# The tokenizer of a vision tower: patches that the host lays out transposed, against patches that the kernel normalises and transposes itself

## The chip, the cores and the metric

The kernel runs on one core of a Trainium2 chip. The metric is the device time of one execution in microseconds. The core's engines are named as the profile names them: PE is TensorE's matmul, PEld its weight load, DVE is VectorE, ACT is ScalarE, POOL is GpSimd, SP is the engine that issues the transfers (DMA). PSUM is the memory of eight banks that PE writes.

## The reference

Sixty-four images of 96 x 96 x 3 are cut into 36 patches of 16 x 16 each, so 2304 tokens; then come three attention layers and a sparse feed-forward layer, which are not touched here. The part at issue is the tokenizer:

```
x5 = concat([x] + shifts(x))            # the image and four copies shifted by one pixel
tokens = patchify(x5, 16)               # 16*16*3*5 = 3840 features a token
mu, var = mean(tokens), mean((tokens - mu)**2)
h = ((tokens - mu) * rsqrt(var + 1e-3) * gamma + beta) @ W + b     # W: 3840 x 192
```

A token and its shifts read one window of 18 x 18 pixels, 972 numbers, each of which occurs in 1, 3, 4 or 5 of the five copies (its count). So the projection over 3840 features can be done over 972 window numbers with a weight that is the sum of five shifted, gamma-scaled weights, and mean and variance are sums over the window weighted by the count.

## The kernel before

The program is one launch in five phases, A to E; `phase_end` makes every engine wait for the other four at the end of each. Phase A is the tokenizer, `phase_tokenizer`. Each engine has a function of its own there (`load` for SP, `vector`, `scalar`, `gpsimd`, `tensor`), works in the order in which it is written, and waits on semaphores.

Before, the tokens of three images (108) are one group, there are 24 groups laid out (22 are real), and six groups are a chunk. The host lays out whole rows of 18 pixels per row of patches (`A_xraw`, 108 partitions, one token row a partition; four transfers, two buffers). For each chunk and each of the six window positions w:

- DVE (`means`, L304) multiplies the window with the counts and sums it; after six of them one small instruction (L310) makes the means.
- ACT (`statistics`, L368) squares the centred window; DVE (`variances`, L320) sums the squares with the counts. There are two buffers of squares, so these two take turns. Ln and Exp (L374, L378) make the reciprocal deviation.
- POOL (L403) normalises the window into `A_xn`, PE transposes it in nine pieces (L427), ACT copies three pieces at a time into `A_xT` (`copies`, L386), and PE projects a group of 108 tokens in nine products (L438). DVE adds the bias (`evacuate`, L329) and writes `h`, which stays on the chip.

Ahead of that, DVE folds the five shifted weights into one (L339, L342: 9 + 36 instructions) while PE multiplies beta with them for the bias (L413, 45 products). In DVE's order this stands behind chunk 0's statistics and ahead of chunk 1's; in PE's order ahead of all transposes. Each fp32 product is two PE records and two PEld records in the trace.

Of the kernel before, what the change touches and what calls it, by code (L numbers as in the profile page):

```python
# [236 lines left out]
def phase_tokenizer(nc, ctx, sem, plan, bank, h, ident, ones, loaded, weights_at):  # L237
# [4 lines left out]
    xraw = [plan(f"A_xraw{s}", [GT, WIN * ROW]) for s in range(2)]  # L242
    xn = [plan(f"A_xn{s}", [GT, WSIZE]) for s in range(3)]
    xT = [plan(f"A_xT{s}", [GT, KT, GT, PER_SIDE]) for s in range(2)]
    count = plan("A_count", [GT, WSIZE])

    sums = [plan(f"A_sums{s}", [GT, 5, PER_SIDE]) for s in range(2)]
    gb = plan("A_gb", [GT, 2, SHIFTS * KT])
    wtok = plan("A_wtok", [GT, KT, DIM])
    bias_bc = plan("A_bias_bc", [GT, DIM])  # L250
    tok_b = plan("A_tok_b", [1, DIM])
    bias_row = plan("A_bias_row", [1, DIM])
    squares = [plan(f"A_squares{s}", [GT, WSIZE]) for s in range(2)]
    scratch = plan("A_scratch", [GT, WSIZE], BF16)
    w5 = plan("A_w5", [GT, SHIFTS, KT, DIM])

    p.ones_set = sem("A_ones_set")
    s_sum, s_mean, s_sq, s_var, s_log, s_rstd = (sem("A_" + n) for n in ("sum", "mean", "sq", "var", "log", "rstd"))
    s_xn, s_T, s_Tev, s_out, s_h = (sem("A_" + n) for n in ("xn", "T", "Tev", "out", "h"))
    s_w, s_bias, s_bias_sb = sem("A_w"), sem("A_bias"), sem("A_bias_sb")  # L260
    slot_load = [loaded["tokx0"], loaded["tokx1"]]
    tbank = bank[0:4]
    obank = bank[4:6]
    bbank = bank[6]

    def window(x, w):

        return x[:, :].rearrange("p (r c) -> p r c", c=ROW)[:, :, PATCH * CHANNELS * w:PATCH * CHANNELS * w + WROW]

    def as_window(t):  # L270
        return t[:, :].rearrange("p (r c) -> p r c", c=WROW)

    def load(sp, ins):
        sp.dma_start(xraw[0][:, :], ins["x"][0]).then_inc(slot_load[0], 16)
        sp.dma_start(count[:, :], ins["count"]).then_inc(loaded["tokc"], 16)
        sp.dma_start(gb[:, :, :], ins["tok_gb"]).then_inc(loaded["tokw"], 16)
        sp.dma_start(tok_b[:, :], ins["tok_b"]).then_inc(loaded["tokw"], 16)
        for k in range(SHIFTS):
            sp.dma_start(w5[:, k], ins["tok_w"][:, k]).then_inc(loaded["tokw"], 16)
            if k == 1:  # L280
                sp.dma_start(xraw[1][:, :], ins["x"][1]).then_inc(slot_load[1], 16)
        for c in range(2, CHUNKS):
            sp.wait_ge(s_xn, PER_SIDE * (c - 1))
            sp.wait_ge(s_sq, PER_SIDE * (c - 1))
            sp.dma_start(xraw[c % 2][:, :], ins["x"][c]).then_inc(slot_load[c % 2], 16)

    def vector(dve):
        dve.wait_ge(loaded["tokc"], 16)  # L290

        def means(c):
            t = sums[c % 2]
            dve.wait_ge(slot_load[c % 2], 16 * (c // 2 + 1))
            for w in range(PER_SIDE):
                if c >= 2:
                    dve.wait_ge(s_rstd, c - 1)

                n = c * PER_SIDE + w
                if n:  # L300
                    dve.wait_ge(s_sum, n)
                    if c:
                        dve.wait_ge(s_var, c * PER_SIDE)
                dve.scalar_tensor_tensor(out=as_window(scratch), in0=window(xraw[c % 2], w), scalar=1.0,  # L304
                                         in1=as_window(count), op0=ALU.mult, op1=ALU.mult,
                                         accum_out=t[:, 0, w:w + 1]).then_inc(s_sum, 1)
            dve.wait_ge(s_sum, PER_SIDE * (c + 1))
            if c >= 2:
                dve.wait_ge(s_xn, PER_SIDE * (c - 1))
            dve.tensor_scalar(t[:, 1, :], t[:, 0, :], -1.0 / FEATS, None, ALU.mult).then_inc(s_mean, 1)  # L310

        def variances(c):
            for w in range(PER_SIDE):
                n = c * PER_SIDE + w
                if w:
                    evacuate(c - 2, w - 1)
                dve.wait_ge(s_sq, n + 1)
                if n:
                    dve.wait_ge(s_var, n)
                dve.scalar_tensor_tensor(out=as_window(scratch), in0=as_window(squares[n % 2]), scalar=1.0,  # L320
                                         in1=as_window(count), op0=ALU.mult, op1=ALU.mult,
                                         accum_out=sums[c % 2][:, 2, w:w + 1]).then_inc(s_var, 1)

        def evacuate(c, j):
            if c < 0:
                return
            n = c * CHUNK_GROUPS + j
# [1 line left out]
            dve.tensor_tensor(h[:, n, :], obank[n % 2][0:GT, 0:DIM], bias_bc[:, :], ALU.add).then_inc(s_h, 1)  # L329

        means(0)
        variances(0)

        dve.wait_ge(loaded["tokw"], 16 * (2 + SHIFTS))
        for k in range(SHIFTS):
            for t in range(KT):
                scale = gb[:, 0, k * KT + t:k * KT + t + 1]
                if k == 0:
                    dve.tensor_scalar(wtok[:, t, :], w5[:, 0, t, :], scale, None, ALU.mult).then_inc(s_w, 1)  # L339
                else:  # L340
                    dve.wait_ge(s_w, (k - 1) * KT + t + 1)
                    dve.scalar_tensor_tensor(out=wtok[:, t, :], in0=w5[:, k, t, :], scalar=scale,  # L342
                                             in1=wtok[:, t, :], op0=ALU.mult, op1=ALU.add).then_inc(s_w, 1)
        dve.wait_ge(s_bias, 1)
        dve.tensor_copy(bias_row[:, :], bbank[0:1, 0:DIM]).then_inc(s_bias_sb, 1)
        dve.wait_ge(s_bias, 2)
        dve.tensor_copy(bias_bc[:, :], bbank[0:GT, 256:256 + DIM]).then_inc(s_bias_sb, 1)
        dve.wait_ge(s_bias_sb, 2)
        means(1)
        variances(1)  # L350
        for c in range(CHUNKS):
            if c + 2 < CHUNKS:
                means(c + 2)
                variances(c + 2)
                evacuate(c, CHUNK_GROUPS - 1)
            else:
                for j in range(CHUNK_GROUPS):
                    evacuate(c, j)

    def scalar(act):  # L360
        def statistics(c):
            t = sums[c % 2]
            act.wait_ge(s_mean, c + 1)
            for w in range(PER_SIDE):
                n = c * PER_SIDE + w
                if n >= 2:
                    act.wait_ge(s_var, n - 1)
                act.activation(as_window(squares[n % 2]), window(xraw[c % 2], w), ACT.Square,  # L368
                               bias=t[:, 1, w:w + 1]).then_inc(s_sq, 1)
                if c:  # L370
                    copies(c - 1, w)
# [1554 lines left out]
```

## Time and profile before

| | |
|---|---|
| median of 3 runs | 1573.12 us (1569.11 to 1573.88) |
| the profiled execution: its time, its span | 1564.85 us, 1562.7 us |
| phase A in it | 0 to 185.65 us |
| busy over the span: PE, DVE, ACT, POOL | 82%, 64%, 60%, 29% |
| granted TensorE clock, mean | 0.92 of full speed |

The span is first to last instruction of the profiled execution; the time of that execution holds a little more. Rows of the trace give a start in us from the span's beginning, a duration, the engine, the kernel's line, and what was written from what. "idle before" is how long the engine stood still ahead of an instruction, and what released it.

### The profile page before, as it was taken

What the parts mean: (1) busy time and instruction counts of PE and PEld (TensorE: products, weight loads), DVE (VectorE), ACT (ScalarE), POOL (GpSimd) and SP (SyncE); (2) the same over time, 40 slices, a digit from 0 to 9 for tenths busy, and PEclk for the clock granted to TensorE, in tenths of its full rate; (3) what the DMA queues carried; (4) which work ended last, traced back from release to release, by engine and by line L of the source; (5) the groups of instructions that cost most, each with busy time, mean ns of one, the idle gap of its engine ahead of it and who ended that gap; (6) DMA issues with size and microseconds to landing.
All of it is one profiled execution on the core that took longest, in us unless ns stands there. A gap on an engine that the chain in (4) does not pass through costs nothing.

```text
span 1562.7 us, 27926 instructions
## 1 busy us (share of the span) xinstructions
PE 1282.7 (82%) x9582; PEld 1164.6 (75%) x9582; DVE 999.2 (64%) x2455; ACT 943.8 (60%) x3298; POOL 458.7 (29%) x447
## 2 busy tenths in 40 slices
PE   1688777778768999999977999999984128999999
PEld 0387776667757888898966888888872117999998
DVE  5663255544546999999866788888875773333333
ACT  2445177777855889889875888888873102222233
POOL 0132100210203233233203334343413304555555
PEclk9688899899977999999998999999996558999999
DMA  5130100020000000000000000000002100000000
GB/s 233 59 117 1 51 12 1 1 62 1 1 1 1 2 1 1 2 1 2 2 10 1 2 1 2 2 1 1 2 2 81 61 0 1 10 1 10 10 10 12
DMA packets 7040, 30.09 MB, mean 19 GB/s; under 512 B 1603, under 2 KB 4400, under 8 KB 5560
## 3 DMA queue, kind: packets, MB, share of 16 engines
q1 hardware_dynamic: 6902, 28.31, 5.6%
q8 instruction: 79, 1.29, 0.3%
q14 instruction: 59, 0.48, 0.1%
HBM read 26.54 MB, written 1.77 MB: 18 GB/s over the span
## 4 chain that ended last, share of the span: by engine, by line
PE 39%; DVE 24%; ACT 4%; issue 3%; POOL 1%; POOLq 0%; ACTq 0%; DVEq 0%
PE bank L1344 4%; DVE t_ss L734 4%; DVE f_eq L1625 4%; DVE t_p L772 3%; PE bank L1370 3%; PE bank L1332 2%; DVE t_raw L750 2%; DVE t_ss L731 2%; PE bank L1312 2%; PE bank L1689 2%; PE bank L1691 2%; PE bank L1704 2%; PE bank L1692 2%; PE bank L1690 2%; PE bank L1693 2%
## 5 line engine op out<-in xcount | busy, mean ns | idle before, releaser
L1164 ACT ACTIVATE t_p<-bank,t_nmax 108x108 f32<-108x108 f32 x792 | 267.4, 355 | 47.6 <-DVE t_nmax L754 46.0
L754 DVE TENSOR_REDUCE t_nmax<-bank 108x4 f32<-108x432 f32 x198 | 119.5, 604 | 141.8 <-PE bank L1344 141.5
L1810 POOL TENSOR_TENSOR f_hid_lo<-f_hid,f_hid_hi 128x432 fp32r<-128x432 f32 (+2 forms) x144 | 145.9, 1014 | 173.5 <-ACT f_hid_hi L1796 173.5
L1013 POOL TENSOR_TENSOR t_sq<-t_raw 108x768 f32<-108x768 f32 x88 | 139.9, 1591 | 181.1 <-ACT t_raw L1104 180.7
L1344 PEld LDWEIGHTS bank<-t_kT,t_qT 128*108 128x108 f32 x1584 | 187.2, 179 | 2.7
L1344 PE MATMUL bank<-t_kT,t_qT 128*108 128x108 f32 x1584 | 187.1, 262 | 0.0
L1766 DVE SCALAR_TENSOR_TENSOR f_hid<-bank,f_maskT 128x432 f32<-128x432 f32 (+2 forms) x144 | 80.2, 557 | 166.9 <-PE bank L1693 165.7
L1796 ACT CAST f_hid_hi<-f_hid 128x432 fp32r<-128x432 f32 (+2 forms) x144 | 73.9, 513 | 182.4 <-DVE f_hid L1766 182.3
L1164 ACT ACTIVATION_READ_ACCUMULATOR t_p<-bank,t_nmax 108x1 f32 x792 | 167.0, 211 | 0.0
L772 DVE TENSOR_TENSOR t_p<-t_p,t_rinv 108x432 f32<-108x432 f32 x198 | 148.9, 752 | 6.8
L1353 PE MATMUL bank<-ident,t_p 108*108 108x108 f32 x792 | 109.6, 261 | 32.6 <-ACT t_xt L1085 28.2
L1021 POOL TENSOR_TENSOR t_xl<-t_xt,t_xh 128x108 fp32r<-128x108 f32 x44 | 18.7, 425 | 330.2 <-DVE t_xh L721 272.4
L1353 PEld LDWEIGHTS bank<-ident,t_p 108*108 108x108 f32 x792 | 82.0, 134 | 44.8 <-ACT t_xt L1085 31.8
L1172 ACT COPY t_pT<-bank 108x432 f32<-108x432 f32 x198 | 99.4, 522 | 16.3 <-PE bank L1353 14.6
L750 DVE TENSOR_TENSOR t_raw<-t_raw,t_rn 108x768 f32<-108x768 f32 x88 | 85.1, 966 | 31.3 <-ACT t_rn L1131 29.1
L1332 PE MATMUL bank<-ident,t_raw 108*128 108x108 f32 x528 | 80.0, 261 | 23.9 <-DVE t_raw L750 11.1
L1104 ACT COPY t_raw<-bank 108x384 f32<-108x384 f32 x176 | 86.3, 493 | 16.0 <-PE bank L1316 15.9
L1332 PEld LDWEIGHTS bank<-ident,t_raw 108*128 108x128 f32 x528 | 62.6, 142 | 42.3 <-ACT t_pT L1172 30.1
L1370 PE MATMUL bank<-t_pT,t_v 108*64 108x108 f32 (+1 forms) x1584 | 86.0, 267 | 1.8 <-issue 1.8
L438 PE MATMUL bank<-A_wtok,A_xT 108*108 108x192 f32 x432 | 81.2, 349 | 6.7 <-ACT A_xT L386 6.7
L1534 PE MATMUL bank<-f_small,f_halves 128*128 128x1 f32 x68 | 19.8, 362 | 78.0 <-DVE f_eq L1625 70.2
L438 PEld LDWEIGHTS bank<-A_wtok,A_xT 108*108 108x108 f32 x432 | 76.0, 188 | 8.5 <-ACT A_xT L386 4.8
(224 smaller groups left out, 3487.6 us busy)
## 6 DMA issues: line engine op xcount, KB each, us to landing
A_xraw<-in_x SPq DMA_DIRECT2D x4, 2232.6 KB
A_w<-in_tok_w SPq DMA_DIRECT2D x5, 729.0 KB
f_raw_down<-in_w_proj SPq DMA_DIRECT2D x1, 2304.0 KB, 8.7
out_tokens<-h SPq DMA_DIRECT2D x21, 81.0 KB
f_raw<-in_w_mfc SPq DMA_DIRECT2D x1, 1536.0 KB, 6.9
f_raw<-in_w_mfc SPq DMA_DIRECT2D x2, 768.0 KB, 11.9
W_raw<-in_wC SPq DMA_DIRECT2D x1, 1159.0 KB
W_raw<-in_wC SPq DMA_DIRECT2D x2, 579.5 KB
```

Source lines behind the costliest of these rows:

```text
L438: mm = pe.matmul(obank[n % 2][0:GT, 0:DIM], xT[c % 2][:, t, rows * j:rows * (j + 1), :].rearrange("p a b -> p (a b)"), wtok[:, t, :], star ...
L750: dve.tensor_tensor(v, v, r, ALU.mult).then_inc(s["qn"], 1)
L754: dve.tensor_reduce(b.nmax[:, 4 * c:4 * c + 4], self.sbank[(3 * g + c) % 2][0:GT, 0:4 * GT].rearrange("p (a n) -> p a n", n=GT), AX.X, ALU ...
L772: dve.tensor_tensor(p, p, b.rinv[:, sl].unsqueeze(2).to_broadcast([GT, 4, GT]), ALU.mult).then_inc(s["pn"], 1)
L1013: pool.tensor_tensor(b.sq[:, 768 * m:768 * m + 768], v, v, ALU.mult).then_inc(s["sq"], 1)
L1164: act.activation(b.p[g % 2][:, m, :], self.sbank[(3 * g + c) % 2][0:GT, n * GT:(n + 1) * GT], ACT.Exp, bias=b.nmax[:, m:m + 1], accum_out= ...
L1172: act.copy(b.pT[:, 4 * c:4 * c + 4, :], src.rearrange("p (a n) -> p a n", a=4)).then_inc(s["Tev"], 1)
L1332: mm = pe.transpose(o, b.raw[k][:, 128 * (3 * u + n):128 * (3 * u + n + 1)], I[0:GT, 0:GT])
L1344: mm = pe.matmul(o[0:GT, n * GT:(n + 1) * GT], b.qT[g % 2][:, hd, :], b.kT[g % 2][:, hd // self.per_tile, :], start=False, stop=True, skip ...
L1353: mm = pe.transpose(t[0:GT, n * GT:(n + 1) * GT], b.p[g % 2][:, 4 * c + n, :], I[0:GT, 0:GT])
L1370: mm = pe.matmul(self.pv[n][lo:hi, t * GT:(t + 1) * GT], b.v[g % 4][:, self.vd * hd:self.vd * (hd + 1)], b.pT[:, hd, :], start=True, stop= ...
L1810: pool.tensor_tensor(self.hid_lo[m % 4][:, c], self.hid[m % 4][:, c], self.hid_hi[m % 4][:, c].bitcast(F32), ALU.subtract).then_inc(s["lo" ...
```

## The change

The host now lays the windows out transposed: window numbers on 121 partitions, eight to a partition (960 of the 972 occur at all, since the window's corners never do; padded to 968 so that all eight numbers of a partition have the same count), tokens along the free dimension, and only the 22 real groups. `A_x` has a buffer for each of six batches (4, 4, 4, 4, 3 and 3 groups), so no load waits for a buffer. Nothing is normalised ahead of the projection:

- `load`: small constants, five weight loads, six batches; the constants `ident`, `owner`, `other` come behind them. The two casts of `owner` and `other` move behind phase A.
- `tensor`: 40 products for the bias and the column sums of the weights (L357), one more (L358), two that spread the results over partitions (L360, L361); then for each group eight products of the raw patches with the weights, 193 columns wide (L370; the last column gives the mean), and one product of one column that sums the squares (L374).
- `vector`: 40 instructions fold the weights (L285, L288), one fills the mean's column (L290), one copies the two rows (L292), one subtracts the weights' column mean, so that the mean of the patch drops out (L295), one copies the bias (L297). For each batch one reduction adds the eight squares of a partition (L304). For each group: copy of mean and mean square (L309), variance (L311), and out of PSUM: times reciprocal deviation plus bias (L316).
- `scalar`: one Square for each batch, which writes in the order of tokens, so with a step of 32 bytes (L335); Ln and Exp for each group (L341, L343).
- `gpsimd`, the transposes, their copies and `A_xraw`, `A_xn`, `A_xT`, `A_count` are gone. `h` shrinks by two groups.

```diff
+BATCHES = [4, 4, 4, 4, 3, 3]
+WT = 8
+WROWS = 121
...
+        pA.load(sp, ins)
         for dst, name in ((ident, "ident"), (owner_f, "owner"), (other_f, "other")):
             sp.dma_start(dst[:, :], ins[name]).then_inc(loaded["const"], 16)
-        pA.load(sp, ins)
...
+        pA.vector(dve)
+        phase_end(dve, "A")
         dve.wait_ge(loaded["const"], 48)
         dve.tensor_copy(owner[:, :], owner_f[:, :]).then_inc(cast_done, 1)
         dve.tensor_copy(other[:, :], other_f[:, :]).then_inc(cast_done, 1)
-        pA.vector(dve)
-        phase_end(dve, "A")
...
+    ld_x = [loaded["tokx0"], loaded["tokx1"], loaded["tokx2"], loaded["tokx2"], loaded["tokx3"], loaded["tokx3"]]
+    of_x = [16, 16, 32, 32, 32, 32]
...
+        dve.scalar_tensor_tensor(out=w[:, :, 0:DIM], in0=wbank[0:WROWS, 0:DIM].unsqueeze(1).to_broadcast([WROWS, WT, DIM]),
+                                 scalar=seen[:, 1:2], in1=w[:, :, 0:DIM], op0=ALU.mult, op1=ALU.add).then_inc(s_w, 1)
...
+        def sum_squares(u):
+            n = BATCHES[u] * GT
+            dve.wait_ge(s_sq, u + 1)
+            if u >= 2:
+                dve.wait_ge(s_out, sum(BATCHES[:u - 1]))
+            dve.tensor_reduce(sums[u % 2][:, 0:n], squares[u % 2][:, 0:n, :], AX.X, ALU.add).then_inc(s_sum, 1)
...
+        dve.wait_ge(s_bias, 1)
+        sum_squares(0)
+        for n, (u, j) in enumerate(groups):
+            if j == 1 and u + 1 < len(BATCHES):
+                sum_squares(u + 1)
+            statistics(n)
+            if n:
+                finish(n - 1)
+        finish(GROUPS - 1)
...
+            act.wait_ge(ld_x[u], of_x[u])
+            if u >= 2:
+                act.wait_ge(s_sum, u - 1)
+            act.activation(squares[u % 2][:, 0:n, :].rearrange("p n t -> p t n"), x[u][:, :, :], ACT.Square)\
+               .then_inc(s_sq, 1)
...
+        square(0)
+        square(1)
+        for n, (u, j) in enumerate(groups):
+            root(n)
+            if j == 1 and u + 2 < len(BATCHES):
+                square(u + 2)
...
+        pe.wait_ge(s_w, CENTRED)
+        for n, (u, j) in enumerate(groups):
+            o, cols = obank[n % 4], slice(j * GT, (j + 1) * GT)
             if j == 0:
+                pe.wait_ge(ld_x[u], of_x[u])
+            if n >= 4:
+                pe.wait_ge(s_h, n - 3)
+            for t in range(WT):
+                pe.matmul(o[0:GT, 0:DIM + 1], x[u][:, t, cols], w[:, t, :], start=(t == 0), stop=(t == WT - 1),
+                          skip_group_check=True)
+            if j == 0:
+                pe.wait_ge(s_sum, u + 1)
+            pe.matmul(o[0:GT, DIM + 1:DIM + 2], sums[u % 2][:, cols], seen[:, 0:1], start=True, stop=True,
+                      skip_group_check=True).then_inc(s_out, 1)
```

PE's order at the start of the program before: the bias products, then all of chunk 0's transposes, then projections and the next chunk's transposes by turns (an x behind a row counts equal neighbours; the figures are rows by columns of the output).

```order
L413 MATMUL bank<-A_w_89,A_gb 1x192 x45
L414 MATMUL bank<-A_tok_b,ones 1x192
L416 MATMUL bank<-A_bias_row,ones 108x192
L427 MATMUL bank<-ident,A_xn_73 108x108 x9
L427 MATMUL bank<-ident,A_xn_74 108x108 x9
L427 MATMUL bank<-ident,A_xn_75 108x108 x9
L438 MATMUL bank<-A_wtok,A_xT_76 108x192 x9
```

The same place after; `A_x_72` and `A_x_73` are the first two batches, `A_sums` the squares summed by partition.

```order
L357 MATMUL bank<-A_w_71,A_gb 2x192 x40
L358 MATMUL bank<-A_tok_b,A_pick 2x192
L360 MATMUL bank<-A_rows,A_pick 128x192
L361 MATMUL bank<-A_rows,A_pick 108x192
L370 MATMUL bank<-A_w,A_x_72 108x193 x8
L374 MATMUL bank<-A_seen,A_sums_80 108x1
L370 MATMUL bank<-A_w,A_x_73 108x193 x8
L374 MATMUL bank<-A_seen,A_sums_81 108x1
```

No transpose is left between the projections, and each group ends in a product that needs DVE's sums. The last pair of rows is the second batch's first group; three more pairs of the first batch stand ahead of it.

ACT's order after, from its first square on: the third batch's square stands ahead of the Ln and Exp of groups 2 and 3.

```order
L335 ACTIVATE A_squares_78<-A_x_72 121x8x432
L335 ACTIVATE A_squares_79<-A_x_73 121x8x432
L341 ACTIVATE A_st_89<-A_st_89 108x1
L343 ACTIVATE A_st_89<-A_st_89 108x1
L341 ACTIVATE A_st_90<-A_st_90 108x1
L343 ACTIVATE A_st_90<-A_st_90 108x1
L335 ACTIVATE A_squares_78<-A_x_74 121x8x432
L341 ACTIVATE A_st_91<-A_st_91 108x1
```

DVE's order after, from the end of the weights to the second group: the sum of the first batch's squares stands behind the centring and the bias, the second batch's ahead of group 1's statistics.

```order
L288 SCALAR_TENSOR_TENSOR A_w<-A_w_71,A_gb,A_w 121x192 x32
L290 COPY A_w<-A_seen 121x8
L292 COPY A_rows<-bank 2x192
L295 SCALAR_TENSOR_TENSOR A_w<-bank,A_seen,A_w 121x8x192
L297 COPY A_bias<-bank 108x192
L304 TENSOR_REDUCE A_sums_80<-A_squares_78 121x432
L309 COPY A_st_89<-bank 108x2
L311 SCALAR_TENSOR_TENSOR A_st_89<-A_st_89 108x1
L304 TENSOR_REDUCE A_sums_81<-A_squares_79 121x432
```

So the weights, which before stood between two chunks' statistics, now come first on DVE, and nothing of the patches is touched ahead of them but ACT's squares.

## Rows read from the trace of the kernel before

**Rows 1.** The page: busy time, share of the span and instructions by engine.

```profile
PE 1282.7 (82%) x9582; PEld 1164.6 (75%) x9582; DVE 999.2 (64%) x2455; ACT 943.8 (60%) x3298; POOL 458.7 (29%) x447
```

**Rows 2.** Timeline where phase A ends: start, duration, engine, line.

```profile
170.67 0.36 DVE L329 TENSOR_TENSOR h<-bank,A_bias_bc 108x192 f32<-108x192 f32 x1 [5.04 <-PE bank L438]
...
185.29 0.36 DVE L329 TENSOR_TENSOR h<-bank,A_bias_bc 108x192 f32<-108x192 f32 x1 [2.57 <-PE bank L438]
185.76 2.02 POOL L527 MEMSET W_rawb<- 33x2318 f32 x1 [29.72 <-DVEq L130]
```

**Rows 3.** Phase A in three stretches: busy time, clock, DMA share, GB/s.

```profile
0.00:52.00 52.00, 18.86 (x105) 9.44 (x106) 31.09 (x76) 8.27 (x9) 3.75 (x7) 1.00 0.44 176
52.00:87.00 35.00, 19.54 (x94) 15.49 (x92) 25.64 (x36) 16.59 (x26) 11.84 (x7) 0.61 0.17 65
87.00:186.00 99.00, 85.58 (x546) 83.02 (x546) 32.24 (x64) 45.41 (x70) 18.14 (x15) 0.91 0.16 47
```

**Rows 4.** Longest waits in phase A: total, times, longest.

```profile
ACT A_squares L368 <- DVE A_sums L310: 71.0, 4, 29.5
DVE h L329 <- PE bank L438: 41.3, 14, 5.0
```

**Rows 5.** DMA share and rate in two stretches (engine columns as in rows 3).

```profile
20.00:30.00 10.00, 0.00 (x0) 0.00 (x0) 8.12 (x15) 6.68 (x7) 0.00 (x0) 1.00 0.74 310
190.00:192.00 2.00, 0.11 (x1) 0.14 (x2) 1.81 (x7) 0.41 (x2) 0.00 (x0) 0.50 1.01 427
```

**Rows 6.** DMA issues at the start, and one transfer's size and landing.

```profile
0.74 0.42 SPq L150 DMA_DIRECT2D ident<-in_ident  x1
3.74 0.97 SPq L279 DMA_DIRECT2D A_w<-in_tok_w  x2
...
ident<-in_ident SPq DMA_DIRECT2D x1, 64.0 KB, 1.7
```

**Rows 7.** The bias products (L413) on PE: first two windows, and all of them.

```profile
34.00:36.00 2.00, 2.00 (x8) 0.84 (x7) 1.00 0.02 4
40.00:42.00 2.00, 2.00 (x14) 1.01 (x12) 1.00 0.00 0
32.70 16.96 PE L413 MATMUL bank<-A_w,A_gb 108*1 108x192 f32 x90 [32.70 <-DMA A_w<-in_tok_w]
```

**Rows 8.** Two projections of nine products each, and the clock around the first.

```profile
86.00:90.00 4.00, 0.96 (x6) 0.72 (x6) 2.72 (x6) 2.66 (x4) 0.00 (x0) 0.79 0.00 0
90.30 5.50 PE L438 MATMUL bank<-A_wtok,A_xT 108*108 108x192 f32 x18
130.41 3.09 PE L438 MATMUL bank<-A_wtok,A_xT 108*108 108x192 f32 x18
```

**Rows 9.** Groups of instructions nearest in kind to the new ones, DVE.

```profile
L342 DVE SCALAR_TENSOR_TENSOR A_wtok<-A_w,A_gb,A_wtok 108x192 f32<-108x192 f32 x36 | 11.9, 404 | 0.0
L503 DVE SCALAR_TENSOR_TENSOR W_raw<-W_mean,W_raw 128x1536 f32<-128x1536 f32 x2 | 3.4, 1724 | 0.0
L499 DVE TENSOR_REDUCE W_mean<-W_raw 128x24 f32<-128x1536 f32 x2 | 3.4, 1719 | 0.0
L731 DVE TENSOR_REDUCE t_ss<-t_sq 108x12 f32<-108x768 f32 x44 | 41.4, 941 | 6.5 <-POOL t_sq L1013 6.5
L734 DVE TENSOR_REDUCE t_ss<-t_sq 108x64 f32<-108x768 f32 x44 | 65.4, 1486 | 6.5 <-POOL t_sq L1013 6.5
```

**Rows 10.** The same on ACT, and one row of PE.

```profile
L1570 ACT CAST f_wd<-f_raw_down 128x4608 fp32r<-128x4608 f32 x1 | 4.0, 4032 | 19.8 <-DMA f_raw_down<-in_w_proj 19.8
63.55 1.91 ACT L386 COPY A_xT<-bank 108x324 f32<-108x324 f32 x3
198.69 1.71 ACT L1149 COPY t_qT<-bank 32x324 f32<-32x324 f32 x4 [0.29 <-PE bank L1330]
L1069 ACT ACTIVATE t_rstd<-t_logv 108x1 f32<-108x1 f32 x66 | 13.4, 203 | 2.1
516.41 0.92 PE L1344 MATMUL bank<-t_kT,t_qT 128*108 128x108 f32 x8
```

More of the change, by code:

```diff
@@ L85, in build_in @@
     fixed = Plan(base)
-    h = fixed("h", [GT, GROUPS_LAID, DIM])
+    h = fixed("h", [GT, GROUPS, DIM])
     ident = fixed("ident", [128, 128])
@@ L131, in phase_end @@
         eng.wait_ge(done, block_engines * (phases.index(name) + 1))
-    pA = phase_tokenizer(nc, ctx, sem, Plan(region), bank, h, ident, ones, loaded, weights_at)
+    pA = phase_tokenizer(nc, ctx, sem, Plan(region), bank, h, ones, loaded)
     prep = weight_prep(nc, sem, Plan(staging_at), loaded, splitC, splitD)
@@ L168, in _ @@
     def _(pe):
-        pe.wait_ge(loaded["const"], 48)
         pA.tensor(pe)
         phase_end(pe, "A")
+        pe.wait_ge(loaded["const"], 48)
         pe.wait_ge(loaded["wB"], 16)
@@ L232, in _, with phase_tokenizer @@
         F.gpsimd_mlp(pool)
-def phase_tokenizer(nc, ctx, sem, plan, bank, h, ident, ones, loaded, weights_at):
+def phase_tokenizer(nc, ctx, sem, plan, bank, h, ones, loaded):
     class A:
@@ L241, in phase_tokenizer @@
     p = A()
[L242 to L271, printed above, removed]
+    w5 = plan("A_w5", [WROWS, SHIFTS, WT, DIM])
+    x = [plan(f"A_x{u}", [WROWS, WT, n * GT]) for u, n in enumerate(BATCHES)]
+    squares = [plan(f"A_squares{s}", [WROWS, BATCHES[0] * GT, WT]) for s in range(2)]
@@ new lines, in phase_tokenizer @@
+    sums = [plan(f"A_sums{s}", [WROWS, BATCHES[0] * GT]) for s in range(2)]
+    w = plan("A_w", [WROWS, WT, DIM + 1])
+    gb = plan("A_gb", [WROWS, SHIFTS * WT, 2])
+    seen = plan("A_seen", [WROWS, 2])
+    tok_b = plan("A_tok_b", [2, DIM])
+    pick = plan("A_pick", [2, 3, 128])
+    rows = plan("A_rows", [2, DIM])
+    bias = plan("A_bias", [GT, DIM])
+    st = [plan(f"A_st{s}", [GT, 5]) for s in range(4)]
+    s_w, s_rows, s_rows_sb, s_wide, s_bias, s_sq, s_sum = (sem("A_" + n) for n in (
+        "w", "rows", "rows_sb", "wide", "bias", "sq", "sum"))
@@ new lines, in phase_tokenizer, with weights_here @@
+    s_out, s_mu, s_var, s_log, s_rstd, s_h = (sem("A_" + n) for n in ("out", "mu", "var", "log", "rstd", "h"))
+    ld_w = [loaded["tokw0"], loaded["tokw1"], loaded["tokw2"]]
+    ld_x = [loaded["tokx0"], loaded["tokx1"], loaded["tokx2"], loaded["tokx2"], loaded["tokx3"], loaded["tokx3"]]
+    of_x = [16, 16, 32, 32, 32, 32]
+    obank = bank[0:4]
+    rbank, wbank = bank[4], bank[5]
+    groups = [(u, j) for u, n in enumerate(BATCHES) for j in range(n)]
+    CENTRED = SHIFTS * WT + 2
+    def weights_here(eng, k):
+        eng.wait_ge(ld_w[k // 2], 32 if k < 4 else 16)
@@ L273, in load @@
     def load(sp, ins):
[L274 to L277, printed above, removed]
+        for dst, name in ((gb[:, :, :], "tok_gb"), (seen[:, :], "tok_seen"), (tok_b[:, :], "tok_b"),
+                          (pick[:, :, :], "tok_pick")):
+            sp.dma_start(dst, ins[name]).then_inc(loaded["tokc"], 16)
@@ L278, in load @@
         for k in range(SHIFTS):
[L279 to L285, printed above, removed]
-    def vector(dve):
[L290 to L327, printed above, removed]
-            dve.wait_ge(s_out, n + 1)
[L329 to L334, printed above, removed]
-        for k in range(SHIFTS):
[L336 to L371, printed above, removed]
-            act.wait_ge(s_var, PER_SIDE * (c + 1))
-            act.activation(t[:, 3, :], t[:, 2, :], ACT.Ln, bias=1e-3, scale=1.0 / FEATS).then_inc(s_log, 1)
-            act.wait_ge(s_log, c + 1)
-            if c >= 2:
-                act.wait_ge(s_xn, PER_SIDE * (c - 1))
-            act.activation(t[:, 4, :], t[:, 3, :], ACT.Exp, scale=-0.5).then_inc(s_rstd, 1)
-        def copies(c, w):
-            for q in range(3):
-                n = (c * PER_SIDE + w) * 3 + q
-                act.wait_ge(s_T, n + 1)
-                if c >= 2:
-                    act.wait_ge(s_out, CHUNK_GROUPS * (c - 1))
-                act.copy(xT[c % 2][:, 3 * q:3 * q + 3, :, w],
-                         tbank[n % 4][0:GT, 0:3 * GT].rearrange("p (t n) -> p t n", t=3)).then_inc(s_Tev, 1)
-        statistics(0)
-        for c in range(1, CHUNKS):
-            statistics(c)
-        for w in range(PER_SIDE):
-            copies(CHUNKS - 1, w)
@@ new lines, in scalar, with square, root @@
+    def scalar(act):
+        def square(u):
+            n = BATCHES[u] * GT
+            act.wait_ge(ld_x[u], of_x[u])
[3 more added lines that the diff above has]
+               .then_inc(s_sq, 1)
+        def root(n):
+            t = st[n % 4]
+            act.wait_ge(s_var, n + 1)
+            act.activation(t[:, 3:4], t[:, 2:3], ACT.Ln, bias=1e-3, scale=-1.0).then_inc(s_log, 1)
+            act.wait_ge(s_log, n + 1)
+            act.activation(t[:, 4:5], t[:, 3:4], ACT.Exp, scale=-0.5).then_inc(s_rstd, 1)
+        square(0)
[4 more added lines that the diff above has]
+                square(u + 2)
@@ new lines, in tensor @@
+    def tensor(pe):
+        pe.wait_ge(loaded["tokc"], 64)
+        for k in range(SHIFTS):
+            weights_here(pe, k)
+            for t in range(WT):
+                pe.matmul(rbank[0:2, 0:DIM], gb[:, k * WT + t, :], w5[:, k, t, :], start=(k + t == 0), stop=False)
+        pe.matmul(rbank[0:2, 0:DIM], pick[:, 0, 0:2], tok_b[:, :], start=False, stop=True).then_inc(s_rows, 1)
+        pe.wait_ge(s_rows_sb, 1)
+        pe.matmul(wbank[0:128, 0:DIM], pick[:, 1, :], rows[:, :], start=True, stop=True)
+        pe.matmul(wbank[0:GT, 256:256 + DIM], pick[:, 2, 0:GT], rows[:, :], start=True, stop=True).then_inc(s_wide, 1)
+        pe.wait_ge(s_w, CENTRED)
+        for n, (u, j) in enumerate(groups):
+            o, cols = obank[n % 4], slice(j * GT, (j + 1) * GT)
+            if j == 0:
+                pe.wait_ge(ld_x[u], of_x[u])
+            if n >= 4:
+                pe.wait_ge(s_h, n - 3)
+            for t in range(WT):
+                pe.matmul(o[0:GT, 0:DIM + 1], x[u][:, t, cols], w[:, t, :], start=(t == 0), stop=(t == WT - 1),
[4 more added lines that the diff above has]
+                      skip_group_check=True).then_inc(s_out, 1)
@@ L453, in phase_tokenizer @@
+    p.load, p.vector, p.scalar, p.tensor = load, vector, scalar, tensor
     return p
@@ L1837, in layouts, with by_row, by_shift @@
     A = {}
-    padded = np.zeros((IMAGES_LAID, SIDE + 2, ROW), f)
-    padded[:IMAGES, 1:-1, CHANNELS:-CHANNELS] = np.asarray(x).reshape(IMAGES, SIDE, SIDE * CHANNELS)
-    xs = np.zeros((CHUNKS, CHUNK_IMAGES, PER_SIDE, WIN, ROW), f)
-    for hh in range(PER_SIDE):
-        xs[:, :, hh] = padded[:, PATCH * hh:PATCH * hh + WIN].reshape(CHUNKS, CHUNK_IMAGES, WIN, ROW)
-    A["x"] = xs.reshape(CHUNKS, GT, WIN * ROW)
-    places = [(1, 1), (1, 0), (1, 2), (0, 1), (2, 1)]
-    def by_window(v):
+    places = [(1, 1), (1, 0), (1, 2), (0, 1), (2, 1)]
+    seen = np.zeros((WIN, WIN), int)
+    for r, c in places:
+        seen[r:r + PATCH, c:c + PATCH] += 1
+    seen = np.repeat(seen.reshape(-1), CHANNELS)
+    at, times = [], []
+    for n in (5, 4, 3, 1):
+        pixels = np.flatnonzero(seen == n)
+        some = np.full(-(-len(pixels) // WT) * WT, -1)
+        some[:len(pixels)] = pixels
+        at.append(some.reshape(-1, WT))
+        times += [n] * len(at[-1])
+    at = np.concatenate(at)
+    assert at.shape == (WROWS, WT)
+    def by_row(v):
+        return np.where((at >= 0).reshape(WROWS, WT, *[1] * (v.ndim - 1)), v[at], f(0))
+    padded = np.zeros((IMAGES_LAID, SIDE + 2, SIDE + 2, CHANNELS), f)
+    padded[:IMAGES, 1:-1, 1:-1] = x
+    tokens = np.stack([padded[:, PATCH * a:PATCH * a + WIN, PATCH * b:PATCH * b + WIN].reshape(IMAGES_LAID, -1)
+                       for a in range(PER_SIDE) for b in range(PER_SIDE)], 1).reshape(GROUPS * GT, -1)
+    xt = by_row(np.ascontiguousarray(tokens.T))
+    ends = np.cumsum([0] + BATCHES) * GT
+    A["x"] = np.concatenate([xt[:, :, a:b].reshape(WROWS, -1) for a, b in zip(ends, ends[1:])], 1)
+    def by_shift(v):
         v = np.asarray(v).reshape(PATCH, PATCH, SHIFTS, CHANNELS, -1)
```

120 lines of the change are left out of this document (47 added, 73 removed).

## The prediction

> **What bounds the kernel now.** I read the page first, to see that no engine is full: PE is busy 82% of the span and DVE 64% [rows 1]. The change touches phase A alone, so I then looked for its end in the timeline: DVE writes the last group's `h` at 185.29 for 0.36, and POOL starts phase B at 185.76 [rows 2]. Phase A is 185.65 us, and whatever leaves it shortens the span one for one, since all engines wait for each other there.
>
> The table of stretches cuts it in three [rows 3]. In the first 52 us PE is busy 18.9 us and DVE 31.1: loads, chunk 0's statistics, then the weights. From 52 to 87 nobody is full, and the clock is 0.61 of full speed. From 87 to 186 PE is busy 85.6 of 99 us. The waits say why: ACT stood 71.0 us in four waits for the means, once 29.5 us [rows 4], and DVE waited 41.3 us for projections. So the first half is a chain DVE, ACT, DVE, POOL, PE, ACT, PE, and the second is PE with transposes between. At the end, where only projections run, a group of nine takes (185.29 - 170.67) / 5 = 2.92 us [rows 2], 0.325 for a product at full clock.
>
> **The change, step by step.** All of the chain goes. What is left is loads, weights, then projections that need nothing but loads and one sum of squares for each batch.
>
> Loads. Issues take some 0.43 us each from 0.74 on [rows 6], so the weights, fifth in the queue, go out at 2.5 and flow from about 3.2. A weight load is 121 x 1536 x 4 = 0.743 MB, the first four batches of patches are 1.673 MB each and the last two 1.254. The rate: 310 GB/s for loads of 108 rows, with 0.74 of the DMA engines busy; 427 for 128 rows with all of them [rows 5]. I take 310, and 1 us for the landing (64 KB took 1.7 in all) [rows 6]. Then the first two weights are there at 9.0, the next two at 13.8, the last at 16.2; the patches of batch 0 at 21.6, batch 1 at 27.0, batches 2 and 3, waited for together, at 37.8, the last at 45.9.
>
> By the Trainium skill (DMA: Bandwidth & Descriptors, "Why a DMA increments its semaphore by 16 and not by 1") a transfer uses the largest number of DMA engines up to 16 that divides its row count: 12 for 108 rows, 16 for 128 and only 11 for 121. The rows agree for the two that they have, 0.74 and 1.01. An estimate by that page is 284 GB/s, which would put the first weights at 9.4 and add 0.4 us to the sum.
>
> The weights. PE does 40 products for the bias. Here it runs cold at first: 8 records in the window from 34 to 36, 14 in that from 40 to 42 [rows 7]; over 90 records in 16.96 us this fits 0.64 us a product for some 4 us and 0.333 after. So 9.1 + 6 x 0.64 + 35 x 0.333 = 24.6 (with the product of L358). DVE folds in 40 x 0.33 = 13.2 us [rows 9], behind the arrivals, and is done by 22.5: hidden under PE. Then copy 0.35 and two products 0.9 (25.9), and the centring, 1536 numbers in the form of L503, 1.72 [rows 9]: 27.7.
>
> The first group. PE has stood still between these steps, much as before 89 us, where the clock had fallen (0.79 in that window) and nine products took 5.50 us for 3.09 [rows 8]. I charge one such loss, 2.4: 27.8 + 8 x 0.327 (193 columns) + 2.4 = 32.8. ACT's square of batch 0: 3456 numbers. Unit step costs 4032 / 4608 = 0.875 ns; with a step of 24 bytes L386 takes 1.91 / 3 = 0.637 us for 324 numbers against 1.71 / 4 = 0.428 for L1149 [rows 10], 0.65 ns a number more. So 1.45 ns and 5.2 us: done at 26.8. The bounds are 3.2 us (unit step) and 1.97 ns, or 6.8 us (all of L386's time by number). DVE copies the bias to 28.1, then sums: from L731 to L499, (1719 - 941) / 768 = 1.01 ns a number [rows 9], so 0.94 + 2688 x 0.00101 = 3.66 us, to 31.8. That is ahead of PE's 32.8. The one-column product: bound by its weight loads; L1344's, with 108 columns, take 0.92 / 4 = 0.23 with the last one's drain [rows 10]. I take 0.2 (0.1 to 0.3): 33.0.
>
> The other 21 groups: 8 x 0.327 + 0.2 = 2.82 each, 59.2: PE ends at 92.2. What stands behind: copy, variance, Ln and Exp at 0.2 each [rows 10] or less, 0.36 for the way out, and handovers, 1.4: phase A ends at 93.6. Does PE go without a stall? In a batch of four groups (11.3 us) ACT has one square and four pairs, 5.2 + 4 x 0.45 = 7.0; DVE 3.66 + 4 x 0.8 = 6.9. ACT's third square stands ahead of group 2's Ln and waits for 37.8, so is done at 43.0; group 2's `h` is then written by 44, and PE needs its bank for group 6, at 33.0 + 5 x 2.82 = 47.1. Covered by 3 us; if the loads came later than 41, group 6 would wait.
>
> At nothing go: POOL's normalising, the transposes and their copies (no longer there), `ident` behind the patches (needed in phase B, there by 55), and the loads of batches 1 to 5, hidden by projections. The two casts, 0.6 us, move from under the loads to ahead of phase B's first DVE work, and PE waits for DVE there: +0.6.
>
> Sum: 185.65 - 93.6 = 92.0 less, 0.6 more, so 91.4 less. The profiled execution took 1564.85, which gives 1473.5. It lies 8.3 below the median of the runs, 1573.12; taken from that, **1482**.
>
> **The rivals.**
> - *DVE's sums become the bound.* L734 sums the same 768 numbers as L731 into 64 results instead of 12, and takes 1486 ns for 941 [rows 9]. It also reads with a large step, the new one doesn't. If the results cost, not the step, that is 545 / 52 = 10.5 ns each: 432 results add 4.5 us, a sum takes 8.2, and DVE has 11.4 us in a batch against PE's 11.3, with the start 4.5 later and the statistics behind each sum late for PE's banks. Phase A would end at 100 to 112: 1488 to 1500. For it: nothing else in the trace sums so few numbers a result. Chance 0.12.
>  The Trainium skill (SBUF — State Buffer, "Specifications (TRN2)") says that accesses which don't hit a 16-byte line at least twice lose rate. By that, L734's extra is its step, and the new sum, which reads in order, keeps 3.7 us; I leave the rival no more than its 0.12 for it.
> - *PE stays at the low clock.* Twenty-two groups at 0.61 a product instead of 0.327 are 22 x 8 x 0.29 = 51 us more: 1533. Against it: from 87 us on, with PE busy 86% of the time and short waits in each group, the clock was 0.91 in the mean [rows 3], and here nothing interrupts it. Chance 0.05.
> - *Slower than before: the loads crowd on few DMA engines.* Twelve of sixteen carried 310 GB/s, some 26 each. All 12.9 MB stand ahead of the last groups; on one engine they take 500 us. The point from which it decides: phase A ends some 9 us after the last batch, so it passes 185 if the rate is below 12.9 MB / 172 us, 75 GB/s, three engines. One engine gives phase A some 530 us and 1573 + 345 = 1918. For it: no transfer of 121 rows is in the trace. Chance 0.03, and the rule above would leave eleven.
> - *Something else in phases B to E moves*, by a clock that falls otherwise at their start or by the addresses that shift with `h`: 5 to 10 us either way, 0.08.
>
> **The numbers.** The forecast has 0.72, with a range of its own from 1475 (no loss of clock, 0.1 for the small product, sums at the lower bounds) to 1490 (0.3 for it, weights late). The range reaches up into the first rival: 1470 to 1503. Within 0.3% is about what a measurement of this kernel can't tell from no change; the cases lie 40 us below or 300 above, so faster 0.96, same 0.01, slower 0.03.
>
> **What would show it.** Phase B's first instruction near 94. PE busy nearly without gap from 33 to 92, groups 2.8 us apart; if the gaps lie at each batch's first group with DVE's sum as releaser, the first rival is right. L304 near 3.7 us (or 8), L335 near 5.2. The first weights at 9, the last patches at 46 to 50. The clock full from about 33 on. I am wrong if PE waits for `h` in every batch, if the loads end behind 60, or if phases B to E are not as long as before.

## The result, and the profile after

| | |
|---|---|
| median after | 1506.62 us (1501.56 to 1511.23, 4 runs) |
| median before, same comparison | 1572.14 us |
| ratio | 0.9585 (0.955 to 0.9619) |
| forecast | 1482 us, 1470 to 1503 |

The change makes the kernel 4.2% faster, 65.5 us by the medians. The forecast was some 90 us, and its range ends at 1503: the direction was right, the size was not. The profiled execution took 1511.23 us.

From the page after: the span and the busy time of the engines, to be held against [rows 1].

```profile
span 1509.2 us, 27177 instructions
PE 1249.7 (83%) x9322; PEld 1136.4 (75%) x9322; DVE 963.7 (64%) x2399; ACT 917.5 (61%) x3244; POOL 425.5 (28%) x423
```

The timeline at the end of phase A (start, duration, engine, line), which answers to [rows 2]: DVE's last write of `h`, POOL's first work of phase B, and the two moved casts.

```profile
123.67 0.42 DVE L316 SCALAR_TENSOR_TENSOR h<-bank,A_st,A_bias 108x192 f32<-108x192 f32 x1 [0.18 <-ACT A_st L343]
124.20 2.03 POOL L451 MEMSET W_rawb<- 33x2318 f32 x1 [123.75 <-DVEq L125]
124.30 2.00 DVE L201 CAST owner<-owner_f 128x108 bf16<-128x108 f32 x1 [0.21 <-DVEq L125]
124.43 2.09 DVE L202 CAST other<-other_f 128x432 bf16<-128x432 f32 x1
```

POOL's first work of phase B comes at 124.20; it was at 185.76. The forecast had 93.6 for the end. What lies behind phase A took 1385.0 us in this profiled execution (1509.2 - 124.2) and 1376.9 in the one before (1562.7 - 185.76). Some 2 of these 8 us are the moved casts, as a run below shows. The rest can't be put down to the change: the profiled execution before lay 8.3 us under its own median, and over the ten profiled executions of this study the stretch takes 1376 to 1387 us.

Phase A is 30.6 us longer than forecast. Where did they go? First five of the longest waits of phase A after (total, times, longest), those that hang on the loads.

```profile
ACT A_squares L335 <- DMA A_x<-in_x: 49.4, 3, 34.6
DVE h L316 <- ACT A_st L343: 25.1, 5, 15.9
DVE A_sums L304 <- ACT A_squares L335: 15.9, 2, 9.6
PE bank L357 <- DMA A_w<-in_tok_w: 14.4, 2, 13.7
PE bank L370 <- DVE h L316: 12.2, 2, 11.5
```

Then the timeline: the weights arrive, the first square and group, the sum of batch 0, the third square, and PE behind its wait.

```profile
13.67 7.31 PE L357 MATMUL bank<-A_w,A_gb 121*2 121x192 f32 x32 [13.67 <-DMA A_w<-in_tok_w]
...
21.73 7.96 PE L357 MATMUL bank<-A_w,A_gb 121*2 121x192 f32 x48 [0.75 <-DMA A_w<-in_tok_w]
...
36.62 6.46 ACT L335 ACTIVATE A_squares<-A_x 121x3456 f32<-121x3456 f32 x1 [34.59 <-DMA A_x<-in_x]
36.73 5.21 PE L370 MATMUL bank<-A_w,A_x 121*108 121x193 f32 x16 [5.28 <-DMA A_x<-in_x]
...
43.18 3.75 DVE L304 TENSOR_REDUCE A_sums<-A_squares 121x432 f32<-121x3456 f32 x1 [9.61 <-ACT A_squares L335]
...
47.37 5.02 PE L370 MATMUL bank<-A_w,A_x 121*108 121x193 f32 x16
...
68.90 6.38 ACT L335 ACTIVATE A_squares<-A_x 121x3456 f32<-121x3456 f32 x1 [10.11 <-DMA A_x<-in_x]
...
76.04 4.36 PE L370 MATMUL bank<-A_w,A_x 121*108 121x193 f32 x16 [11.49 <-DVE h L316]
...
80.36 2.85 PE L370 MATMUL bank<-A_w,A_x 121*108 121x193 f32 x16
...
83.17 2.85 PE L370 MATMUL bank<-A_w,A_x 121*108 121x193 f32 x16
```

Every step that stands on a load is late, and each by more than the one ahead: weights 13.7 instead of 9.0, batch 0 at 36.6 instead of 21.6, batches 2 and 3 at 68.9 instead of 37.8. ACT stands in front of the third square, and the Ln and Exp of group 2 come behind it in ACT's order. So DVE waits 15.9 us for them, and PE 11.5 us for the bank that DVE should have freed. From 80 us on the groups start 2.81 us apart, as forecast.

Two stretches, to be held against [rows 5]: the first weights on their way, and PE's long stand. The last three columns are the granted clock, the share of the DMA engines that were busy, and GB/s.

```profile
4.00:12.00 8.00, 0.00 (x0) 0.00 (x0) 0.00 (x0) 0.00 (x0) 0.00 (x0) 1.00 0.70 179
72.00:76.00 4.00, 0.00 (x0) 0.00 (x0) 0.43 (x2) 3.78 (x5) 0.00 (x0) 0.50 0.89 198
```

The loads ran at 179 GB/s, not 310, with 0.70 of the engines busy: eleven of sixteen, each at 16 GB/s. Before, twelve moved 26 each. And while PE stood, its clock was at 0.50, the lower of its two levels (1.2 and 2.4 GHz), so the group behind the stand took 4.36 us and not 2.85.

### The profile page after: what moved, and what is told of

Its sections match the earlier page's. It is cut to its first block, busy times and chain, and to the rows that moved or that the text cites. A ratio compares the mean times of both kernels' runs of the same rounds, so it can differ in the third digit from the quotient of the medians.

```text
span 1509.2 us, 27177 instructions
## 1 busy us (share of the span) xinstructions
PE 1249.7 (83%) x9322; PEld 1136.4 (75%) x9322; DVE 963.7 (64%) x2399; ACT 917.5 (61%) x3244; POOL 425.5 (28%) x423
## 4 chain that ended last, share of the span: by engine, by line
PE 41%; DVE 25%; ACT 4%; issue 3%; POOL 1%; POOLq 0%; ACTq 0%; DVEq 0%
PE bank L1268 4%; DVE t_ss L658 4%; DVE f_eq L1549 4%; DVE t_p L696 4%; PE bank L1294 3%; PE bank L1256 3%; DVE t_raw L674 3%; DVE t_ss L655 2%; PE bank L1236 2%; PE bank L1613 2%; PE bank L1628 2%; PE bank L1615 2%; PE bank L1614 2%; PE bank L1616 2%; PE bank L1617 2%
## 5 line engine op out<-in xcount | busy, mean ns | idle before, releaser
L1277 PE MATMUL bank<-ident,t_p 108*108 108x108 f32 x792 | 109.1, 260 | 31.1 <-ACT t_xt L1009 26.7
L370 PE MATMUL bank<-A_w,A_x 121*108 121x193 f32 x352 | 68.1, 352 | 17.4 <-DVE h L316 12.2
L1458 PEld LDWEIGHTS bank<-f_small,f_halves 128*128 128x128 f32 x68 | 16.9, 312 | 82.6 <-DVE f_eq L1549 72.8
```

Of the source, the lines that this page charges most:

```text
L1277: mm = pe.transpose(t[0:GT, n * GT:(n + 1) * GT], b.p[g % 2][:, 4 * c + n, :], I[0:GT, 0:GT])
```

## The experiments

The question was why eleven engines move only 16 GB/s each. Three theories. **P, placement**: a transfer is cut into blocks of neighbouring rows, one block for each engine (eleven rows each of 121), and engines whose rows at a moment lie behind the same port of the on-chip memory share one engine's rate, 427 / 16 = 26.7 GB/s. **S**: this layout's pieces in the device memory are slow to read, for any rows. **Count alone**: only the number of engines matters, each with 26 GB/s; it would have given 284, so the result itself speaks against it.

The map for P is the Trainium skill's (SBUF — State Buffer, "Door 1: The DMA port swizzle"): a port serves four rows, and the same four moved by 32. By that map the first rows of 121 / 11 blocks (0, 11, 22 and so on) lie behind seven ports, those of 99 / 11 behind eleven, of 108 / 12 behind twelve, of 120 / 15 behind eight. Which engine takes which rows no row of the trace shows; the block order is an assumption that the runs test. An estimate with it and the page's map follows all loads through their engines from 3.2 us on, at 26.7 GB/s for an engine and for a port and with nothing added for the landing. It puts the first two weight loads at 12.4, batch 0 at 36.9 and batch 3 at 68.8 us, where the trace has 13.7, 36.6 and 68.9.

**128 rows** (`e1_rows128`): buffers and host arrays of weights and patches get seven rows of zeros, the computing stays on 121.

```diff
-    w5 = plan("A_w5", [WROWS, SHIFTS, WT, DIM])
-    x = [plan(f"A_x{u}", [WROWS, WT, n * GT]) for u, n in enumerate(BATCHES)]
+    w5 = plan("A_w5", [128, SHIFTS, WT, DIM])
+    x = [plan(f"A_x{u}", [128, WT, n * GT]) for u, n in enumerate(BATCHES)]
...
-    A["tok_w"] = by_shift(L0_tok_W)
+    A["tok_w"] = full_rows(by_shift(L0_tok_W))
```

> The weights and the patches are moved as 128 rows (seven rows of zeros more, 13.7 MB instead of 12.9); nothing else changes. Theory P (placement): a transfer of 121 rows runs on 11 DMA engines with 11 neighbouring rows each, and engines whose rows lie behind the same port of the memory share one engine's rate, 26.7 GB/s (427 GB/s over 16, from the loads of 128 rows before). Then 128 rows run at some 420 GB/s, batch 3 is there at 30 us instead of 69, PE has no long wait left, phase A ends at 92 to 94 instead of 123.7, and the median is 1474 to 1478. Theory S (slow source): the pieces of this layout are read at 16 GB/s by each engine whatever the rows. Then 128 rows run at 256 GB/s, batch 3 is there at 47, phase A ends near 101, and the median is some 1484. Theory N: the rate is not what costs; phase A ends above 115.

Measured: median 1480.37 us, some 2 us above what I expected, ratio to before 0.942 (0.9366 to 0.9473). Its stretch from 4 to 12 us, then its first squares, its first group, and the start of phase B.

```profile
4.00:12.00 8.00, 3.64 (x12) 1.53 (x13) 3.67 (x14) 0.00 (x0) 0.00 (x0) 1.00 1.01 419
```

```profile
18.04 12.77 ACT L335 ACTIVATE A_squares<-A_x 121x3456 f32<-121x3456 f32 x2 [16.01 <-DMA A_x<-in_x]
27.16 5.48 PE L370 MATMUL bank<-A_w,A_x 121*108 121x193 f32 x16 [1.91 <-DVE A_w L295]
32.69 2.94 PE L370 MATMUL bank<-A_w,A_x 121*108 121x193 f32 x16
93.50 2.03 POOL L451 MEMSET W_rawb<- 33x2318 f32 x1 [93.05 <-DVEq L125]
```

More bytes, and 2.3 times the rate: 419 GB/s. Phase A ends at 93.5, 30.7 us earlier than with 121 rows, and behind the first weights no wait of PE for a load or for DVE's `h` is left. So the whole shortfall of phase A against the forecast comes from the loads. S is out (256 GB/s). P is not yet shown: a theory that counts engines, all sixteen here, gives the same. And P as it stands has a hole here: by the block order the first rows of 128 / 16 blocks (0, 8, 16 and so on) lie behind only eight ports too, which would be 214 GB/s. With 128 rows the rows must be dealt out to the engines in some other way than in blocks; no run shows how.

**108 + 13, 99 + 22, 120 + 1 rows**: each load is split in two by rows, same bytes at the same addresses (for 99 + 22 all five weight loads of 99 rows go first). The numbers that the semaphores wait for double with it.

```diff
-            sp.dma_start(w5[:, k], ins["tok_w"][:, k]).then_inc(ld_w[k // 2], 16)
+            for a, b in ROWS_OF:
+                sp.dma_start(w5[a:b, k], ins["tok_w"][a:b, k]).then_inc(ld_w[k // 2], 16)
```

> Each load of weights and patches is split into one of 108 rows and one of 13, same bytes, same addresses. Theory P: 12 engines of nine rows each meet no shared port (310 GB/s before), the 13 single rows lie behind four ports; the mix comes to some 225 GB/s, batch 3 at 50 us instead of 69, phase A ends near 104. Theory S: 12 engines of 16 GB/s are 190 GB/s, batch 3 at 62, phase A near 116.

> Each load is split into 99 rows and 22 rows; both go on 11 engines as the 121 did. The five weight loads of 99 rows go first. Theory P: with nine rows an engine the 11 engines meet no shared port, so the rate from 4 to 12 us is 280 to 294 GB/s, against 165 to 190 with 121 rows in that stretch; the loads of 22 rows behind them are slow again, the mean over all is near 194. Theory S, and a theory by which the number of engines alone sets the rate: 165 to 190 from 4 to 12 us too, with 0.69 of the engines busy in either.

> Each load is split into 120 rows and one. 120 rows go on 15 engines, eight rows each. Theory P: the 15 engines reach only eight ports at a time, so four more engines than the 121 rows had bring 200 GB/s at 0.94 of the engines busy; batch 3 at 55 us, phase A ends near 109. A theory by which the number of engines sets the rate gives 15 x 26.7 = 400 GB/s; theory S gives 240.

The stretch from 4 to 12 us of each. First 108 + 13:

```profile
4.00:12.00 8.00, 0.52 (x2) 0.24 (x3) 0.56 (x3) 0.00 (x0) 0.00 (x0) 1.00 0.80 272
```

99 + 22, where only 99-row loads run in that stretch:

```profile
4.00:12.00 8.00, 0.00 (x0) 0.00 (x0) 0.00 (x0) 0.00 (x0) 0.00 (x0) 1.00 0.69 275
```

120 + 1:

```profile
4.00:12.00 8.00, 0.03 (x1) 0.06 (x2) 0.06 (x1) 0.00 (x0) 0.00 (x0) 1.00 0.96 222
12.00:20.00 8.00, 8.00 (x32) 3.45 (x33) 4.83 (x17) 0.00 (x0) 0.00 (x0) 1.00 0.96 214
```

The pair 121 and 99 decides against S and the count. Both run on eleven engines (0.70 and 0.69 busy), read the same array, and differ in the rows: 121 give 179 GB/s, 99 give 275. And 120 rows keep fifteen engines busy (0.96) for only 214 to 222 GB/s, 14 to 15 each: four engines more than 99 rows have, and a lower rate. Eight ports at 26.7 are 214. For 121, 99 and 120 rows theory S has 176, 176 and 240, the count alone 284, 284 and some 400; each misses at least one. P, as put down ahead of the runs, has 165 to 190, 280 to 294 and 200, within some tenth of all three. The 108 + 13 mix ran at 217 to 272 over its stretches of 8 us; P had some 225 as the mean, S 190. Behind its first stretch 99 + 22 ran at 205 to 255, faster than P's mean of 194.

The traces also keep a record of every row moved, with its time. These are the rows of the weights (6144 bytes each) that start from 4 to 12 us:

| rows of a load | records | of at most 250 ns | median |
|---|---|---|---|
| 128 | 546 | 542 | 234 ns |
| 99 | 358 | 300 | 235 ns |
| 121 | 233 | 21 | 393 ns |
| 120 | 289 | 16 | 448 ns |

With 128 rows practically every row takes 234 ns, which is 26.3 GB/s. Some rows of the 121 take no longer, so the layout in the device memory isn't in itself slow to read. With 120 rows nine records in ten stay under 484 ns, about twice 234, as if two engines shared one rate; P has fifteen engines on eight ports there. So it is shown that the row count of a load sets its rate, and not the engines' number or the layout. That engines share ports by the map is argued, from rates that it gave ahead of the runs, and the way in which 128 rows are dealt out stays open.

The times of these three follow the loads: phase A ends at 106.9, 107.0 and 116.7 us by POOL's first row, for forecasts of 104 (108 + 13) and 109 (120 + 1). The second was 7.7 us out: its third square started at 60.35, where batch 3 was expected at 55, and PE's group behind the wait for it took 5.36 us at the low clock. The times are of one run each, 1488.34, 1490.63 and 1497.76 us, in the order of phase A's end.

**A semaphore for each batch** (`e5_own_sems`), with 121 rows: is PE's 11.5 us wait ACT's place behind the pairwise wait, or the loads?

```diff
-    ld_x = [loaded["tokx0"], loaded["tokx1"], loaded["tokx2"], loaded["tokx2"], loaded["tokx3"], loaded["tokx3"]]
-    of_x = [16, 16, 32, 32, 32, 32]
+    ld_x = [loaded[f"tokx{u}"] for u in range(6)]
+    of_x = [16] * 6
```

> 121 rows as in the changed kernel, but each of the six batches has a semaphore of its own, so the third square waits for batch 2 alone. If the 11.5 us in which PE waits for a bank at 64.5 come from ACT's place behind that pairwise wait, the square of batch 2 starts at 58 to 60 instead of 68.9, PE waits some 1 to 2 us instead of 11.5, and phase A ends at 113 to 116 instead of 124. With the loads at 175 GB/s the fourth square then waits for batch 3 at 69, which is hidden. If PE's wait is the loads themselves (theory L: PE needs batch 3 or later at that time), nothing changes.

Measured: 1499.42 us, ratio to before 0.9535 (0.9509 to 0.9562), against 0.9585 (0.955 to 0.9619) for the changed kernel, so some 8 us by the ratios, with intervals that overlap a little. The timeline shows the mechanism: third square, PE's longest wait, start of phase B.

```profile
59.45 6.45 ACT L335 ACTIVATE A_squares<-A_x 121x3456 f32<-121x3456 f32 x1
66.66 2.88 PE L370 MATMUL bank<-A_w,A_x 121*108 121x193 f32 x16 [1.58 <-DVE h L316]
114.24 2.02 POOL L451 MEMSET W_rawb<- 33x2318 f32 x1 [113.79 <-DVEq L125]
```

The square starts 9.5 us earlier, PE's longest wait for a bank is 1.6 us, and with no long stand PE also keeps its clock (2.88 us for the group, not 4.36). Phase A is 10 us shorter. So a third of the loss came through the order on ACT, and it exists only while the loads are slow: with 128 rows and the pairwise wait still in place PE waited for no bank.

**The casts ahead of the phase's end** (`e7_casts_early`).

```diff
+        dve.wait_ge(loaded["const"], 48)
+        dve.tensor_copy(owner[:, :], owner_f[:, :]).then_inc(cast_done, 1)
+        dve.tensor_copy(other[:, :], other_f[:, :]).then_inc(cast_done, 1)
         phase_end(dve, "A")
-        dve.wait_ge(loaded["const"], 48)
-        dve.tensor_copy(owner[:, :], owner_f[:, :]).then_inc(cast_done, 1)
-        dve.tensor_copy(other[:, :], other_f[:, :]).then_inc(cast_done, 1)
```

> The changed kernel with the two casts ahead of the end of phase A instead of behind it. Theory C: the casts take 2.0 us each there because POOL fills a buffer at the same time; ahead of the phase's end POOL stands still, so they take 0.22 and 0.38 us as in the kernel before, and from phase A's end to PE's next product it is some 6.2 us instead of 8.3. Theory D: they are slow for another reason (their place behind the long phase, the data just landed); then they take 2 us here too.

One run, 1504.08 us. The casts, POOL's first fill, and PE's first product of phase B.

```profile
121.93 0.20 DVE L200 CAST owner<-owner_f 128x108 bf16<-128x108 f32 x1
122.05 0.38 DVE L201 CAST other<-other_f 128x432 bf16<-128x432 f32 x1
122.53 2.02 POOL L451 MEMSET W_rawb<- 33x2318 f32 x1 [122.08 <-DVEq L125]
128.67 0.77 PE L1212 MATMUL bank<-ident,t_xf 108*128 108x108 f32 x3 [8.03 <-DVE t_xf L631]
```

0.20 and 0.38 us instead of 2.00 and 2.09, and 6.1 us from POOL's start to PE's product; with 128 rows and late casts it was 8.3 (93.50 to 101.78). Theory C holds: the casts still stand behind the long phase, and only POOL's fill beside them is gone. The Trainium skill (SBUF — State Buffer, "Who interferes with whom") has the rule, that a cast in DVE's fast two-port mode and a POOL instruction take turns as wholes on a shared pair of ports. The changed kernel's rows agree: the fill ended at 126.23, the casts at 126.30 and 126.52.

**The step of the squares** (`e8_unit_step`), with 128 rows. ACT now writes one number behind the other, and DVE's sum reads with a step of 1728 bytes instead.

```diff
-    squares = [plan(f"A_squares{s}", [WROWS, BATCHES[0] * GT, WT]) for s in range(2)]
+    squares = [plan(f"A_squares{s}", [WROWS, WT, BATCHES[0] * GT]) for s in range(2)]
```

> 128 rows, and the squares are written in the order of the patches (step of one number); DVE's sum reads them with a step of 1728 bytes instead. If the step of 32 bytes is what makes the square 6.46 us, it takes 3.1 to 3.3 us now. The sum, 3.75 us before, should take 6.5 to 6.9 if a stepped read costs 1.93 ns a number as in L734. DVE then has about 10 us of work for a batch of 11.3, and phase A ends 1 to 4 us later than with 128 rows alone, at 94 to 97. If ACT's own rate were the limit, the square stays at 6.4.

One run, 1480.81 us, which by itself can't be told from 128 rows alone; phase B starts at 97.14, 3.6 us later than there. One square in the timeline, and DVE's sums (minimum, median, maximum ns).

```profile
18.25 3.08 ACT L335 ACTIVATE A_squares<-A_x 121x3456 f32<-121x3456 f32 x1 [16.22 <-DMA A_x<-in_x]
```

```profile
L304 DVE TENSOR_REDUCE A_sums<-A_squares x6: 4544/5975/6015, 28.5 to 82.3; 121x432 f32<-121x3456 f32 x4, 121x324 f32<-121x2592 f32 x2
```

The step doubled the square: 6.46 us with it, 3.08 without. DVE's sum went from 3.75 to 5.98 us, less than the 6.5 to 6.9 expected. The work only moved from an engine that nobody waits for to the one ahead of PE, and phase A is 3.6 us longer: the changed kernel has the step on the right side.

**All that helps** (`e6_rows128_sems_casts`): 128 rows, own semaphores, early casts.

> 128 rows, own semaphores, and the two casts back ahead of the end of phase A. At 420 GB/s the pairwise wait should cost nothing, so the semaphores bring nothing here; the casts take some 0.6 us inside phase A instead of 2.2 behind it. Phase A ends near 94.2, PE's first work of phase B comes some 6.2 us behind it instead of 8.3, and the median lies 1 to 2 us below that of the kernel with 128 rows alone, 1478 to 1480; against the kernel before a ratio near 0.94.

Median 1475.44 us (1472.82 to 1478.01), some 3 us below what I expected, ratio to before 0.9389 (0.9363 to 0.9415). It beats the changed kernel, whose ratio is 0.9585; against 128 rows alone (0.942, 0.9366 to 0.9473) the intervals overlap, and only the timeline (phase B at 94.49, PE's first product 6.1 us later at 100.62, not 8.3 later) shows the casts' 2 us, of which 1.2 are left net (100.62 against 101.78), since phase A ends 1.0 us later.

## Why the prediction was wrong

- **The step that failed is the rate of the loads** ("I take 310, and 1 us for the landing"). Measured: 179 GB/s. I had the rates of two transfers, of 108 and of 128 rows, took the one of 108 for 121, and for the estimate took the rate to go with the number of busy engines. For those two it does, among 121, 99 and 120 rows it doesn't. What stands in its place by the runs: the row count of a load can halve the rate of every engine; that they crowd at ports is the likely reason, not shown to the end. The rule that I weighed was right in what it says: 0.70 of the engines is eleven. My use of it, 284 GB/s and 0.4 us, was not. And the range held nothing for it: between 284 GB/s and the rival's 75 no rate had a price or a chance.
- **The sum breaks in two places.** The first group ended at 47.3 instead of 33.0: 14.3 us, and batch 0's load is 15.0 late. Then 11.5 us in PE's wait for group 6's bank. The working had named the point ("if the loads came later than 41, group 6 would wait"): they came at 68.9. With 2.2 and 1.5 us for the clock after these stands and 0.7 for a short wait this makes 30.2 of the 30.6 that phase A is over.
- **The rivals.** "The loads crowd on few DMA engines" had the right place and the wrong question, how many engines are at work instead of how fast each of them is. Its point of decision, 75 GB/s, was not reached, so the sign held. PE's low clock cost three groups (5.21, 5.02, 4.36 us), not all. DVE's sums are cheap: 3.75 us, forecast 3.66; that rival is out. Of the rival that phases B to E move nothing is shown beyond the casts. Of the signs of being wrong, one came: the loads ended behind 60.
- **Right in mechanism and size:** groups 2.81 us apart (2.82), the centring 1.82 (1.72), one loss of clock at the first group (5.48 us in the run with 128 rows, 5.0 charged). **Mis-sized:** the square, 6.46 for 5.2 us, inside its bounds and hidden (its 1.45 ns a number is also a slip, the two terms beside it make 1.52, which is what 5.2 us needs; measured 1.87); the casts, over 2 us on the path instead of 0.6, since the two that I priced from under the loads now run beside POOL's fill.
- With fast loads the rest of the sum stands: with 128 rows phase A ends at 93.5, forecast 93.6, and the median is 1480.37, forecast 1482. That both agree so closely is partly luck. The loads ran at 419 GB/s there, not 310; this gave only 0.6 us, since PE waits for the first weights alone (8.4 for 9.0), and the first group's 5.48 us for 5.0 took most of it back. In the total the casts cost 1.6 us more than charged, well inside the noise.

## What to carry to other kernels

Before a layout is given a row count, measure a transfer with it: here 121 rows moved 179 GB/s, 120 rows some 215, 99 rows 275, 108 rows 310, and 128 rows, seven of them zeros, 419. Seven useless rows were worth 26 us. When a forecast prices a transfer of a shape that the trace doesn't have, the range has to take in half the nearest rate, and each waiting instruction that is queued ahead of others (here ACT's third square) has to be followed with that late arrival. Where two batches share one semaphore, the first waits for the second; one for each was worth 10 us of phase A here.
